# High parts and rests of a half tile in one instruction each over two PSUM banks, and the output bank copied by ScalarE and summed by GpSimd

## What is computed

```python
q = apply_rope(q)
k = apply_rope(k)
logits = jnp.einsum('bhid,bhjd->bhij', q, k) * SCALE
logits = jnp.einsum('bhij,gh->bgij', logits, Wpre)
attn = jax.nn.softmax(logits, axis=-1)
attn = jnp.einsum('bhij,gh->bgij', attn, Wpost)
out = jnp.einsum('bhij,bhjd->bhid', attn, v)
out = out.transpose(0, 2, 1, 3).reshape(b, n, DIM)
return out @ Wout.T + bout
```

## Time and profile before

| | before |
|---|---|
| median of 3 runs | 8362.6 us (8351.86 to 8367.09) |
| profiled execution | 8358.64 us, its span 8356.8 us |
| mean granted TensorE clock | 0.984 of full speed |
| busy share of the span | PE 96%, DVE 91%, ACT 82%, POOL 72% |

### The profile page before, as it was taken

How to read it: one execution, slowest core, us unless ns; L and a number is a source line. 1 busy time by engine, 2 the same in 40 slices (tenths; PEclk the granted TensorE clock), 3 DMA queues, 4 the chain that set the end, 5 groups by cost and what they waited for, 6 DMA issues and landing times.

```text
span 8356.8 us, 449859 instructions
## 1 busy us (share of the span) xinstructions
PE 7996.8 (96%) x182764; PEld 4649.9 (56%) x182764; DVE 7605.1 (91%) x13390; ACT 6848.0 (82%) x11648; POOL 6046.9 (72%) x12006
## 2 busy tenths in 40 slices
PE   7999999998899999999889999999979999999997
PEld 4555555555555555555545555555554555555554
DVE  7999999997899999999789999999978999999996
ACT  5888888886688888888568888888857888888884
POOL 6777777774677777777477777777737777777773
PEclk9999999998999999999899999999989999999998
DMA  1011111112101111111211111111121011011112
GB/s 53 23 28 27 26 26 27 26 27 91 34 24 27 27 26 26 27 28 26 89 35 25 26 27 26 27 26 27 26 88 36 25 26 28 25 27 26 27 26 93
DMA packets 265756, 284.04 MB, mean 34 GB/s; under 512 B 41089, under 2 KB 252673, under 8 KB 261377
## 3 DMA queue, kind: packets, MB, share of 16 engines
q1 hardware_dynamic: 263680, 255.07, 11.3%
HBM read 78.75 MB, written 39.85 MB: 14 GB/s over the span
## 4 chain that ended last, share of the span: by engine, by line
PE 73%; DVE 12%; issue 10%; POOL 1%; ACT 1%; DVEq 1%; DMA 0%; SPq 0%; POOLq 0%; ACTq 0%
PE psS L1248 47%; PE psP L1267 15%; PE psO L1282 6%; DVE big L878 5%; DVE pl L906 2%; DVE spare L867 2%; PE psM L1293 1%; ACT big L694 1%; DVE ot L889 1%; PE psS L1378 1%; PE psM L1308 1%; PE psS L1407 1%; PE psS L1209 0%; DVE nb L867 0%; PE psS L1196 0%
## 5 line engine op out<-in xcount | busy, mean ns | idle before, releaser
L1248 PE MATMUL psS<-KH,AX 64*128 64x512 f16 x32768 | 3928.4, 377 | 52.0 <-DMA AX<-AX 50.1
L694 ACT ACTIVATE big<-psP 128x512 f16<-128x512 f32 x4096 | 2222.4, 595 | 826.2 <-PE psP L1267 822.9
L878 DVE SCALAR_TENSOR_TENSOR big<-psP,big 128x512 f16<-128x512 f32 x4096 | 2613.9, 679 | 175.5 <-ACT big L694 174.0
L675 ACT ACTIVATE pr<-psS,nb 128x1024 f32<-128x1024 f32 x2048 | 2289.7, 1118 | 192.9 <-DVE nb L867 190.1
L1248 PEld LDWEIGHTS psS<-KH,AX 64*128 64x128 f16 x32768 | 1451.5, 95 | 1513.5 <-DMA AX<-AX 51.7
L704 ACT ACTIVATE ph<-pr 128x1024 f16<-128x1024 f32 x2048 | 2166.8, 1058 | 32.3
L1248 PE MATMUL psS<-KL,AX 64*128 64x512 f16 x16384 | 2106.3, 377 | 0.0
L906 DVE TENSOR_TENSOR pl<-pr,ph 128x1024 f16<-128x1024 f32 (+1 forms) x2048 | 2078.3, 1015 | 0.0
L1267 PE MATMUL psP<-rh,ph 64*128 64x64 f16 x32768 | 1671.7, 191 | 131.4 <-DVE big L878 112.0
L1267 PEld LDWEIGHTS psP<-rh,ph 64*128 64x128 f16 x32768 | 1468.7, 95 | 557.9 <-DVE big L878 395.9
L1267 PE MATMUL psP<-rl,ph 64*128 64x64 f16 x32768 | 1667.0, 191 | 4.7 <-issue 4.3
(11 more groups left out here) (137 smaller groups left out, 6286.4 us busy)
## 6 DMA issues: line engine op xcount, KB each, us to landing
AX<-AX SPq DMA_DIRECT2D x2048, 64.0 KB, 2.0
ph<-in_xT SPq DMA_DIRECT2D x16, 512.0 KB, 8.7
xr<-in_x SPq DMA_DIRECT2D x64, 128.0 KB, 2.3
Q<-in_w SPq DMA_DIRECT2D x8, 1024.0 KB, 7.2
out<-V SPq DMA_DIRECT2D x16, 512.0 KB, 3.7
d_x<-x SPq DMA_DIRECT2D x60, 128.0 KB, 2.0
d_xn<-xn SPq DMA_DIRECT2D x60, 128.0 KB, 2.0
d_lg<-lg SPq DMA_DIRECT2D x60, 128.0 KB, 2.0
```

Of the source, the lines that this page charges most:

```text
L675: a.activation(pr[:, p, h * N2:(h + 1) * N2], psS[:, 2 * h:2 * h + 2, :].rearrange("p c n -> p (c n)"), ACT.Exp, bias=nb[:, p, h:h + 1], s ...
L694: a.activation(PT[:, hf * JH:(hf + 1) * JH, :, 0, i0:i0 + HQ], psP[:, ih, :].rearrange("p (j g i) -> p j g i", j=JH, g=H), ACT.Copy, scale ...
L878: v.scalar_tensor_tensor(out=PT[:, js, :, 1, i0:i0 + HQ], in0=psP[:, ih, :].rearrange("p (j g i) -> p j g i", j=JH, g=H), scalar=MDROP, in ...
L1248: mm = pe.matmul(psS[:, 2 * hp + half, :], AX[rows, k8, kq, s_, :], K_[rows, kq, hp, :], start=n == 0, stop=n == len(steps) - 1, tile_posi ...
```

## The change

The layout of `PT` is changed so that both banks of `psP` can be read and written by one instruction: the 8 tiles' queries are now stored as two runs of 32, the first four queries of each tile and the last four. `mixed_high` is one ACT instruction over 1024 numbers in place of two over 512, and `mixed_low` one DVE instruction in place of two. Which queries a tile holds is changed in `mixq` to match (two runs of four, 32 apart). The output products read `PT` in four runs of 32 in place of one of 128. The two reductions of DVE in slots 3 and 11 are gone; ACT copies the whole bank `psO` to a new buffer `oraw` between its second high parts and its second exponentials, and POOL adds the two halves behind its `pl` part. Only the last half group of each batch is still added by DVE (`out_copy`).

```diff
-        PT = big[:, :].bitcast(F16).rearrange("p (j g s i) -> p j g s i", j=JT, g=H, s=2)
+        PT = big[:, :].bitcast(F16).rearrange("p (f h j g s i) -> p f h j g s i", f=2, h=2, j=JH, g=H, s=2)
...
+        oraw = sb("oraw", [P, GQ * P])
...
-                        i0 = it * (TI * QI) + (t * QI + h * HQ)
+                        i0 = it * (TI * QI) + t // TG * GI + h * (GI // 2) + t % TG * HQ
...
+                def out_sum(n, half, R):
+
+                    g.wait_ge(s_or, b * (NIT * 2 - 1) + n + 1)
+                    g.wait_ge(s_y, R + 1)
+                    parts = oraw[:, :].rearrange("p (q h s i) -> p q h s i", q=GQ, h=2, s=2)
+                    apart(g)
+                    g.tensor_tensor(ot[:, :, half * GI:(half + 1) * GI].rearrange("p q (h i) -> p q h i", h=2),
+                                    parts[:, :, :, 0, :], parts[:, :, :, 1, :], ALU.add).then_inc(s_oc, 2)
...
-                def mixed_high(T, t, c, Gd):
-
-                    hf, ih = c // 2, c % 2
+                def mixed_high(T, t, hf, Gd):
+
                     a.wait_ge(s_D, T * 2 + hf + 1 + 1)
                     if t % TG == 0:
                         a.wait_ge(s_F, Gd * NC + 2 * hf + 2)
-                    i0 = (t % TG) * QI + ih * HQ
-                    a.activation(PT[:, hf * JH:(hf + 1) * JH, :, 0, i0:i0 + HQ],
-                                 psP[:, ih, :].rearrange("p (j g i) -> p j g i", j=JH, g=H),
+                    i0 = (t % TG) * HQ
+                    a.activation(PT[:, hf, :, :, :, 0, i0:i0 + HQ].rearrange("p h j g i -> p (h j g) i"),
+                                 psP[:, :, :].rearrange("p h (a i) -> p (h a) i", i=HQ),
                                  ACT.Copy, scale=MDROP).then_inc(s_mh, 1)
+
+                def out_raw(n):
+
+                    Gd = b * (NIT * 2) + n
+                    a.wait_ge(s_F, (Gd + 1) * NC + NC)
+                    a.wait_ge(s_oc, Gd * 2 + 1)
+                    a.activation(oraw[:, :], psO[:, :], ACT.Copy).then_inc(s_or, 1)
...
                     mixed(0)
-                    mixed(1)
                     if live:
                         exps(T, t, 0, early)
                         highs(T, t, 0, early)
...
-                    mixed(2)
-                    mixed(3)
+                    mixed(1)
+                    if t % TG == 3 and not (first and t < TG) and it < NIT:
+                        out_raw(it * 2 + t // TG - 1)
...
-                def mixed_low(T, t, c):
-
-                    v.wait_ge(s_mh, T * NC + c + 1 + 1)
-                    hf, ih = c // 2, c % 2
-                    i0 = (t % TG) * QI + ih * HQ
-                    js = slice(hf * JH, (hf + 1) * JH)
-                    v.scalar_tensor_tensor(out=PT[:, js, :, 1, i0:i0 + HQ],
-                                           in0=psP[:, ih, :].rearrange("p (j g i) -> p j g i", j=JH, g=H),
-                                           scalar=MDROP, in1=PT[:, js, :, 0, i0:i0 + HQ],
-                                           op0=ALU.mult, op1=ALU.subtract).then_inc(s_ml, 1)
+                def mixed_low(T, t, hf):
+
+                    v.wait_ge(s_mh, T * 2 + hf + 1 + 1)
+                    i0 = (t % TG) * HQ
+                    high, rest = (PT[:, hf, :, :, :, k, i0:i0 + HQ].rearrange("p h j g i -> p (h j g) i") for k in range(2))
+                    v.scalar_tensor_tensor(out=rest, in0=psP[:, :, :].rearrange("p h (a i) -> p (h a) i", i=HQ),
+                                           scalar=MDROP, in1=high, op0=ALU.mult, op1=ALU.subtract).then_inc(s_ml, 1)
...
                     if two:
                         mixed_low(T - 2, t_2, 0)
-                        mixed_low(T - 2, t_2, 1)
-                    copied(it, t, first, 0)
...
-                        mixed_low(T - 2, t_2, 2)
-                        mixed_low(T - 2, t_2, 3)
-                    copied(it, t, first, 1)
+                        mixed_low(T - 2, t_2, 1)
```

More of the change, by code:

```diff
@@ L259, in seq_layer @@
         s_oc = sem("s_oc")
+        s_or = sem("s_or")
         s_xr = sem("s_xr")
@@ L622, in slot @@
                         low(T - 1, t_1, first and t < 3)
+                    if t % TG == 3 and not (first and t < TG) and it < NIT:
+                        out_sum(it * 2 + t // TG - 1, (t // TG + 1) % 2, b * NIT + it - (1 if t < TG else 0))
                     roots(it, t, 2)
@@ L729, in slot, with mixed @@
                     early = first and t < 2
-                    def mixed(c):
+                    def mixed(hf):
                         if not (first and t < 2):
-                            mixed_high(T - 2, (t - 2) % TI, c, G + (t - 2) // TG)
+                            mixed_high(T - 2, (t - 2) % TI, hf, G + (t - 2) // TG)
                     mixed(0)
-                    mixed(1)
                     if live:
@@ L888, in out_copy @@
                     qs = slice(part * GQ // 2, (part + 1) * GQ // 2)
-                    ins = v.tensor_reduce(ot[:, qs, half * GI:(half + 1) * GI],
-                                          psO[:, qs.start * P:qs.stop * P].rearrange("p (q s i) -> p q i s", s=2, i=GI),
+                    ins = v.tensor_reduce(ot[:, qs, half * GI:(half + 1) * GI].rearrange("p q (h i) -> p q h i", h=2),
+                                          psO[:, qs.start * P:qs.stop * P].rearrange("p (q h s i) -> p q h i s", h=2, s=2, i=GI // 2),
                                           X, ALU.add)
@@ L1022, in combine @@
                     v.tensor_scalar(ew[:, :], ew[:, :], er[:, 0:1], None, ALU.mult).then_inc(s_C, 1)
[L1024 to L1028, removed]
                 def rows(it, t, place):
@@ L1260, in turn @@
                     if not fresh:
-                        pe.wait_ge(s_ml, T * NC + 2 * hf + 1)
+                        pe.wait_ge(s_ml, T * 2 + hf + 1)
                     for j in range(JH):
@@ L1276, in output @@
                     for c in pieces:
-                        pe.wait_ge(s_ml, Tn * NC - NC + c // 2 * 2 + 2 + 1)
+                        pe.wait_ge(s_ml, Tn * 2 - 2 + c // 2 + 1 + 1)
                         for j in range(c * JC, (c + 1) * JC):
@@ L1282, in output @@
                                     mm = pe.matmul(psO[32 * w:32 * w + 32, q * P:(q + 1) * P],
-                                                   V[:, j, g_, :, :], PT[:, j, g_, :, :],
+                                                   V[:, j, g_, :, :], PT[:, j // JH, :, j % JH, g_, :, :],
                                                    start=j == 0 and q == 0, stop=j == JT - 1,
```

## The result

The changed kernel takes 8473.1 us (median of 4; 8468.7 to 8478.2) against 8364.9: ratio 1.0133, 95% interval 1.0115 to 1.0150, 108 us slower. The prediction was 8430, slower. The profiled execution has a span of 8469.7 us, 112.9 more than before.

What follows compares the result with a forecast made beforehand. TensorE (96% busy) was taken to pace plain slots, the ACT-DVE ring just hidden; merging would put the ring above it. 116 - 12 - 42 + 6 = +68 us on 8358.6 gives 8427, predicted as 8430; range 8320 to 8530.

Steps and rivals of the forecast that it cites:

- The ring: ACT-DVE wait cycle once per plain slot (one tile): 6.41 us becomes 6.80, 0.22 over PE's 6.58; 528 slots, 116 us.
- the two paths: Chains setting a plain slot: 6.80 us through ScalarE's exponentials and ph, 6.77 through TensorE's turn, both through the second rest.
- M0 to L0: VectorE, first half (0): from start of the maximum (M) to start of the rests (L), taken as 1.22 us.
- L0 to turn 1: First half's rests on VectorE to TensorE's second turn: the rests' own 1.22 us, then 0.06 to the turn.
- H1 to L1: Second half (1): ScalarE's high parts (H) to VectorE's rests (L), start to start; 0.63 us would become 1.09.
- L1 to l0: VectorE: second half's rests to first half's pl (l), start to start; 1.20 us would become 1.13.
- The head start: PE can run ahead about 0.1 us before stalling, once in each of 124 runs of plain slots: -12 us.
- What is gained behind the output products: Slots 10 to 12 and 2 to 4, DVE-paced: moved sums and merged rests gain 0.35 us per stretch, about 120 stretches, -42 us.
- The tails: A batch's two closing slots, where nothing hides high part, rest and turn: +6 us over four batches.
- Copy and sum: ACT's output-bank copy (0.595 us) and GpSimd's sum (671 ns) cost next to nothing; uncovered 60 and 83 us; that rival 10%.
- VectorE's work: Merged rests save DVE 0.07 us per half, 143 us in all; the skill's bubble figure gave 0.125 a merge, 256 us.
- A sign that failed: PE's turns waiting for DVE's rests would rise from 219 pieces to over 500.

Runs made afterwards that it cites:

- e3: Changed kernel with the second half's high parts and rests again one instruction per bank, the first half's merged: 8364.9 us, ratio 0.9998 to the kernel before.
- e6: Changed kernel with high parts merged but rests again one instruction per bank in both halves: 8541.8 us, ratio 1.0207 to the kernel before.
- e5: Changed kernel with high parts again one instruction per bank but rests merged in both halves: 8531.0 us, ratio 1.0196 to the kernel before.
- e1: Changed kernel with high parts and rests again one instruction per bank in both halves, sums still moved: 8318.1 us, ratio 0.9948 to the kernel before.
- e8: Changed kernel plus one 128x64 VectorE addition between pl and the next maximum: 8580.7 us, ratio 1.0256 to the kernel before.
- e9: Changed kernel plus one 128x64 VectorE reciprocal between the second maximum and the second rest: 8525.0 us, ratio 1.0195 to the kernel before.
- e2: Changed kernel, still merged, but output bank summed by DVE as before, without ACT's copy and GpSimd's sum: 8494.9 us, ratio 1.0159 to the kernel before.
- e12: e11 with ScalarE's output-bank copy in slot 11 also moved behind ph: 8317.4 us, ratio 0.9948 to the kernel before.
- e11: e1 with GpSimd's sum of the first half group moved from slot 11 to 15: 8314.7 us, ratio 0.9940 to the kernel before.

## Why the prediction was right, and where it was off

**The ring: right, and its size too.** 6.80 us was worked out, 6.81 measured, and the excess of 0.22 is 0.23. That the hundredths agree is partly luck. Of the two paths that I gave, ScalarE's (6.80) is not the one that decides but PE's, for which I had 6.77. Its steps in the rows above: M0 to L0 1.21, L0 to turn 1 1.35, turn 1 to H1 0.91, H1 to L1 1.06, L1 to l0 1.14, l0 to M0 1.14, together 6.81. H to L is 1.06 where I took 1.09: the high part lasts 1.025 us, less than the 1.058 that I had called the floor. From the rest's end to the turn it is 0.15 where the earlier trace rows had 0.06. Here too a wait moved: in the changed kernel the wait for `s_ml` ahead of turn 1 stands in an instruction of its own, and in the kernel before and in e3 to e6 the first load carries it, so the load starts 0.12 us behind the rest's end in place of 0.05. Against e5, whose high parts are released in the same way, H1 comes 0.02 us later behind the rest's end (1.06 for 1.04), so the moved wait is a small part of the 0.23. e1 shows that the merging is the cause, and e1 beside e6, which merges the high parts alone, that it is the wait of the first rest for the whole high part; e5 and e6 that it is not the length of either instruction; e8 and e9 that only time inside the ring counts.

**The head start: wrong, -12 us that is not there.** All eight intervals grew in full, the last of each run (into the output slot) too: 1.86 us a group by medians and 1.97 by means, with the first groups 123 to 129 us in all (60 groups, and 12 x 0.23 us in each of four first groups). The slack of 0.1 us was real, for the first load stood 0.10 us ahead of its product; the error, as I read it now, was to count it once in each run. H1 waits for turn 1, so the ring starts anew at every turn 1, at the time that PE itself reached, and the next one comes 6.81 us later at once. The traces fit this: from the last score product to the first product of turn 1 the median is 0.44 us already in slot 7, the first of a run, 0.43 in those behind it, and was 0.21 in all of them.

**What is gained behind the output products: too large, -42 us that are about -14 to -23.** It is 0.24 us a group by means and 0.39 by medians, times 60. It is half a matter of the merge: with both halves split the slots 2 to 4 and 10 to 12 give back 1.30 us a group by the table (48.40 to 47.10), of which 0.31 is lost again in 13 and 14. In the changed kernel slot 3 is 6.91 in place of 6.58 and slot 11 7.34 in place of 7.06, and so they are in e2, without the moved sums. The same wait for the high parts stands in these slots too, and I had counted it once, at the first high part, and not at those behind it; that this is all of it was not traced wait by wait.

**The sum again.** By means it is 129 us of plain slots in place of 116 - 12 = 104, and -14 in place of -42: 115 us beside the 112.9 by which the span grew, where I had 68. The tails, put at +6, don't show: in three of four batches the stretch from the last maximum to the next batch or the end is 0.5 to 1.9 us shorter, and the one that is 5.6 longer is as much longer in e1, which merges nothing.

**Copy and sum: near enough.** The copy takes 0.591 us and is covered (e12). The sum takes 0.726 (I took 0.671), and was not free: 0.31 us a group in e1, and in the changed kernel slot 12 takes 6.75 us where e2, without the sum, has 6.65. VectorE's `pl` beside it is held up, and GpSimd's next instruction by `pl` in turn. GpSimd's timeline, then DVE's, in slot 11:

```profile
1032.04 0.73 POOL L516 TENSOR_TENSOR ot<-oraw 128x256 f32<-128x256 f32 x1
1032.72 1.18 POOL L530 TENSOR_TENSOR zr<-zr,vr 128x2 f32<-128x2 f32 x1
```

```profile
1032.39 1.45 DVE L922 TENSOR_TENSOR pl<-pr,ph 128x1024 f16<-128x1024 f32 x1
```

1.45 us in place of 1.21 for `pl`, and 1.18 for two numbers a partition. That this holds for e11's 0.39 us too was not traced instruction by instruction.

**VectorE's work: right in kind.** L to l is 1.14 from start to start in place of 1.18 to 1.20, half or less of the 0.125 us that the prediction worked out, as an estimate, from the Trainium skill (VectorE: DVE Perf Modes, the TRN2 errata). The two savings of a slot do lie on the path, L0's own 0.07 us (1.27 to 1.20) and L1's 0.06, and the 6.81 has them in it. They are small beside the 0.43 by which the first rest starts later, so more saved work of this kind would not have turned the sign.

**A sign that failed.** I had said that the turns' waits for DVE would rise from 219 pieces to over 500. They fell to 166, for 79.6 us: the chain shows the new loss as "issue" and as a longer turn, and the list of waits has it on the weight loads, 736.3 us in 1650 pieces for VectorE's rests and "issue" together, where it was 433.9 in 1015. I had named the wrong row. The wait of the rest for the high part rose as forecast, from 174.0 us to 494.0.

## What to carry to other kernels

Two instructions on two banks are also a pipeline between two engines: before merging them, close the ring of waits once with the second engine's start moved to the first one's end, and compare its length with the engine that sets the pace. If the ring comes out longer, the merge costs the difference in every slot, and work taken from an engine that is 91% busy is worth little where that engine waits. An experiment that changes how much an instruction adds to a semaphore has to be looked at in its own trace before its time is read: e3 to e6 paid 0.06 to 0.07 us a merged instruction for it. Here the other half of the change alone, the output bank copied by ScalarE and summed by GpSimd, is the better kernel: 8318 us, 0.5% under the one before.

## What the runs showed that was not expected

A turn that waited for VectorE's rest starts on time in the chain and takes 0.79 us in place of 0.70, or 0.88 when the rest is later still; the wait stands on its weight loads, which start 0.05 us behind the rest's end. A merged instruction that adds 2 to its semaphore has its wait in an instruction of its own ahead of it and starts 0.10 us behind what it waits for; where it adds 1 it starts 0.03 to 0.04 behind. A VectorE addition of 128x64 with both inputs in SBUF took 0.98 us on average beside a GpSimd instruction and 0.22 without, and a reciprocal of 128x64 takes 0.54. Why the changed kernel's wait for `s_ml` stands apart from the first load, and that of the kernel before does not, stays open.
